# A 32-head attention layer and its feed-forward part on one core: output product from float16 pairs, first head by tiles, bounds' transfers on ScalarE's queue, new orders

## The chip, the core and the metric

The kernel runs on one core of a Trainium2 chip. A core has a matmul engine (TensorE, PE in the profile), a vector engine (VectorE, DVE), a scalar engine (ScalarE, ACT), a general engine (GpSimd, POOL) and a queue engine (SyncE, SP) that here issues nothing but transfers. Each engine works through its own instructions strictly in order, and they wait for one another by semaphores. The matmul engine reads its operands from the on-chip memory SBUF and writes to the accumulator memory PSUM, from which VectorE and ScalarE fetch the results. The metric is the device time of one execution in microseconds (us).

## The reference, cut to what matters

```python
x = hidden_states                       # (1, 1024, 512) float32
q  = layernorm(x) @ wq                  # 32 heads; 128 of each head's 192 columns are used
k, v = layernorm(x) @ wkv               # 32 heads of 128 each
probs = softmax(causal(q @ k.T * 192 ** -0.5))
x = x + (probs @ v for all heads, side by side) @ wo      # wo: (4096, 512)
h = relu(s0 * (layernorm(x) @ w0)) * 2  # w0, w1, w2: (512, 512) of +1 and -1
h = relu(s1 * (scaled(h) @ w1)) * 2
out = x + s2 * (scaled(h) @ w2)
```

## The kernel before

Tokens stand in 8 tiles of 128 (NT), and in 2 halves of 512 (NC). Every product is made from pairs: an operand is split into a high part (its float16 rounding) and a low part (the rest), and high by high, high by low and low by high are added up in PSUM. So a product of 128 contracted rows is 3 matmuls. Only the output product of attention (`project_out`, tiles `wos` and `attn`) and the feed-forward part use pairs of float32r values, which are four bytes wide.

The heads go in 16 groups of two (`GH`, `j` is the head in its group). Per head there are: seven products of the Strassen-Winograd scheme for q and k (`x1` to `x7`, 6 matmuls of 512 columns each), eight rows of scores (`s0` to `s7`, 128 to 1024 columns wide, 3 matmuls per 512 columns), four projections of values (`v`, 12 matmuls of 256 columns, eight a group since they serve both heads), two products of probabilities and values (`pv0`, `pv1`: 12 and 24 matmuls), and eight output tiles (`o0` to `o7`, 3 matmuls of 512 columns). In lots of 512 columns a group is 84 + 54 + 48 + 54 + 48 = 288.

Around them work: VectorE finds a score row's scaled minimum (`m`, line 968), takes the low part of the exponentials (`l`, line 975), gathers the products into q and k (`a`, line 907), takes the low part of values (`v`, line 952) and of attention (`pv`, line 958), adds the output to the residual (`o`, line 991), and works out a power of two by which the weights are scaled (`sc`, lines 930 to 941). ScalarE does exponentials (`e`, 706), high parts (`h` 714, `qk` 699, `v` 720, `pv` 728), the copy of the first product (`snap`, 655), sums of squares of the weights (`mx`, 688) and their scaling (`r`, 674). GpSimd splits the weights (`wqk`, `wv`, `wo`: lines 484, 487, 542, 545), forms the sums of weights of the scheme (`sum`, ten instructions), and the low parts of q and k (`qk`, 536). SyncE loads weights, transposes the probabilities by DMA (`t`, 460), and sends the sums of squares to DRAM and back, spread over the partitions (`put`, 405, `get`, 412).

What stands in which place on each engine is written out by hand as five tables of words (`TENSOR_ORDERS` and so on): `o7@-1` is output tile 7 of the head before the group's first, `x2@2` product 2 of the head two further on. The first string is the group that repeats, the second what stands ahead of group 0. Scores use two halves of one part of PSUM in turn (`psS`): row n waits for `l` of row n-2. All other products share four banks (`psC`), handed out by `BANKS` in the order of the products: a product waits in `bank_free` until whoever fetches the bank's last contents is done, with `a`, `snap`, `v`, `pv` or `o`.

## Time and profile before

| | us |
|---|---|
| median of 3 runs | 1137.72 |
| lowest, highest | 1137.38, 1139.09 |
| the profiled execution's own time | 1138.74 |
| its span in the trace | 1136.9 |
| PE busy in it | 1092.0 |
| DVE, ACT, POOL busy | 895.9, 678.0, 667.6 |

A matmul's duration in the trace includes the time until its result has drained, and the next one starts before it ends. So PE's pace is read from starts, not from durations, and its idle time is a little more than what the trace calls idle. Instructions of VectorE and ScalarE overlap a little too: a follower that waits for nothing starts about 0.08 to 0.10 us ahead of the end of the one before it.

### The profile page before, as it was taken

To read this page: it belongs to the slowest core of one execution; us is meant where nothing else is said; L and a number is where in the kernel's file an instruction comes from. 1 tells how busy PE (TensorE), PEld (TensorE's weight loads), DVE (VectorE), ACT (ScalarE), POOL (GpSimd) and SP (SyncE) were. 2 spreads that over 40 slices of the span, in tenths; PEclk is the share of its full clock that TensorE was granted. 3 is DMA by queue.
4 is the path that set the end of the run, shared out by engine and by line. 5 is a ranking of instruction groups with operands and counts; after the bars stand their busy time and mean duration, and the time that the engine had idled before them with its cause. 6 is when DMAs were issued, how large, how long until landed. Compare 5 with 4: busy or idle time off the path is not lost.

```text
span 1136.9 us, 18752 instructions
## 1 busy us (share of the span) xinstructions
PE 1092.0 (96%) x6223; PEld 655.2 (58%) x6223; DVE 895.9 (79%) x1797; ACT 678.0 (60%) x1334; POOL 667.6 (59%) x682
## 2 busy tenths in 40 slices
...
GB/s 157 88 99 84 119 108 128 100 116 94 96 112 109 121 114 114 82 117 109 91 121 114 124 82 119 112 76 121 117 130 89 117 107 81 118 93 115 92 1 75
DMA packets 367584, 118.25 MB, mean 104 GB/s; under 512 B 313088, under 2 KB 361344, under 8 KB 367488
## 3 DMA queue, kind: packets, MB, share of 16 engines
...
q8 instruction: 50, 0.82, 0.3%
q14 instruction: 46, 0.38, 0.2%
...
## 4 chain that ended last, share of the span: by engine, by line
PE 75%; DVE 12%; issue 6%; ACT 4%; POOL 3%; DMA 0%; SPq 0%; POOLq 0%; ACTq 0%; DVEq 0%
PE psC L1108 42%; PE psS L1108 16%; PE psC L1231 16%; DVE p L975 3%; DVE qk L907 2%; POOL wqk L487 2%; ACT raw L674 2%; POOL wqk L484 1%; DVE res L991 1%; DVE attn L958 1%; ACT attn L728 1%; DVE bound L930 1%; DVE psS L968 0%; DVE bound L936 0%; DVE bound L933 0%
## 5 line engine op out<-in xcount | busy, mean ns | idle before, releaser
L1108 PE MATMUL psC<-xb,wqk 128*128 128x512 f16 x1356 | 328.1, 381 | 12.5 <-POOL wqk L487 10.9
L706 ACT ACTIVATE psS<-psS,negmax 128x128 f32<-128x128 f32 (+7 forms) x256 | 182.8, 714 | 221.3 <-DVE negmax L968 220.4
L1108 PE MATMUL psC<-wos,attn 128*128 128x512 f32 x768 | 253.5, 441 | 13.5 <-DVE attn L958 10.1
L968 DVE CUSTOM_DVE_ANT_0 psS<-psS,mask,undo_qk 128x128 f32<-128x128 f32 (+7 forms) x256 | 208.4, 820 | 62.2 <-PE psS L1108 60.5
L975 DVE SCALAR_TENSOR_TENSOR p<-psS,p 128x128 f16<-128x128 f32 (+7 forms) x256 | 192.6, 752 | 60.2 <-ACT p L714 57.1
L1108 PE MATMUL psS<-qkT 128*128 128x512 f16 (+3 forms) x1152 | 230.0, 327 | 1.2 <-DVE p L975 0.7
L1108 PEld LDWEIGHTS psC<-xb,wqk 128*128 128x128 f16 x1356 | 124.5, 98 | 160.3 <-issue 36.3
L1231 PE MATMUL psC<-pT,v 128*128 128x512 f16 (+3 forms) x1152 | 197.8, 326 | 0.0
L991 DVE SCALAR_TENSOR_TENSOR res<-psC,rinv,res 128x512 f32<-128x512 f32 x256 | 190.1, 743 | 9.3 <-DVE rinv L982 8.1
L1108 PE MATMUL psC<-wvs,xb 128*128 128x256 f16 x1536 | 188.5, 273 | 0.4 <-POOL wvs L487 0.4
L484 POOL TENSOR_TENSOR wqk<-raw,one 128x512 f16<-128x512 f32 x122 | 115.9, 950 | 110.4 <-ACT raw L674 97.8
L714 ACT ACTIVATE p<-psS 128x128 f16<-128x128 f32 (+7 forms) x256 | 166.3, 649 | 17.9 <-DMA pT<-p 0.3
L1108 PEld LDWEIGHTS psC<-wos,attn 128*128 128x128 f32 x768 | 137.2, 190 | 63.4 <-issue 22.9
L536 POOL TENSOR_TENSOR qkT<-qk,qkT 128x512 f16<-128x512 f32 x120 | 137.1, 1158 | 59.6 <-ACT qkT L699 59.6
L1108 PEld LDWEIGHTS psC<-wvs,xb 128*128 128x128 f16 x1536 | 147.6, 98 | 35.8 <-issue 4.4
L1231 PEld LDWEIGHTS psC<-pT,v 128*128 128x128 f16 x1152 | 108.6, 98 | 91.5 <-DVE qk L907 4.1
L1108 PEld LDWEIGHTS psS<-qkT 128*128 128x128 f16 x1152 | 97.8, 98 | 102.9 <-issue 34.4
L487 POOL TENSOR_TENSOR wqk<-raw,wqk 128x512 f16<-128x512 f32 x124 | 129.1, 1041 | 15.8 <-ACT wqk L693 6.2
L484 POOL TENSOR_TENSOR wvs<-raw,one 128x512 f16<-128x512 f32 x45 | 46.8, 1040 | 119.3 <-ACT raw L674 82.3
L907 DVE SCALAR_TENSOR_TENSOR qk<-psC,qk 128x512 f32<-128x512 f32 x120 | 95.5, 816 | 10.0 <-PE psC L1108 8.4
L699 ACT ACTIVATE qkT<-qk 128x512 f16<-128x512 f32 x120 | 73.5, 625 | 38.2 <-DVE qk L907 38.2
L720 ACT ACTIVATE v<-psC 128x256 f16<-128x256 f32 x128 | 48.6, 381 | 62.0 <-PE psC L1108 62.0
...
## 6 DMA issues: line engine op xcount, KB each, us to landing
...
pT<-p SPq DMA_TRANSPOSE x256, 4.3
wrow<-wmax_rows SPq DMA_DIRECT2D x45, 64.0 KB, 4.7
...
```

The lines of the kernel that those rows point to most:

```text
L484: nc.gpsimd.tensor_tensor(hi, src, one[:, :].to_broadcast([P, src.shape[1]]), ALU.mult) \
L487: nc.gpsimd.tensor_tensor(lo, src, hi, ALU.subtract).then_inc(lo_sem, 1)
L536: nc.gpsimd.tensor_tensor(lo, qk32[:, AT[n], :], hi, ALU.subtract) \
L699: nc.scalar.activation(qkT[:, qk_slot(j, n), HI, :], qk32[:, AT[n], :], ACT.Copy) \
L706: nc.scalar.activation(row, row, ACT.Exp, bias=negmax[:, n:n + 1], scale=-1.0, accum_out=rowsum[:, j % 2, n:n + 1]) \
L714: nc.scalar.activation(parts_of(n)[:, :, HI, :], psS[:, n % 2, 0:(n + 1) * P].rearrange("p (k s) -> p k s", s=P), ACT.Copy, scale=UP).then ...
L907: nc.vector.scalar_tensor_tensor(to, product, OUT_DOWN, base32, ALU.mult, ALU.add).then_inc(gathered[n], 1)
L968: nc.vector.tensor_tensor_reduce(row, row, mask[:, S - width:S], undo_qk[:, j % 2:j % 2 + 1], 3e38, ALU.add, ALU.min, negmax[:, n:n + 1]). ...
L975: nc.vector.scalar_tensor_tensor(parts[:, :, LO, :], psS[:, n % 2, 0:(n + 1) * P].rearrange("p (k s) -> p k s", s=P), UP, parts[:, :, HI, ...
L991: nc.vector.scalar_tensor_tensor(res[:, t, :], psC[:, bank, :], rinv[:, t:t + 1], res[:, t, :], ALU.mult, ALU.add).then_inc(added, 1)
L1108: last = nc.tensor.matmul(out_ap, w, x, start=k == 0, stop=k == len(terms) - 1)
L1231: last = nc.tensor.matmul(o, a, b, start=(kt == 0 and k == 0), stop=(kt == count - 1 and k == 2))
```

## The change

- The output product reads float16 pairs. `wos` and `attn` are float16. The weights of the output are now scaled by a power of two as those of q, k and v are: their sum of squares (`mx2`), the bound (shared with that of the values, two columns at once) and the scaling (`r2`) come on top. ScalarE first copies a `pv` product to a float32 tile (`pv`, which frees the bank), then makes the high part from it (`ah`); the low part (`al`) goes from VectorE to GpSimd. The factor that undoes the scaling moves into the inverse of the row sums (one more small instruction per head on VectorE).
- `put` and `get` move from SyncE's queue to ScalarE's. Both output weights of a pair are loaded together.
- The first head's q and k are made tile by tile (128 columns) for four of the eight products, each as soon as its tile of x is there, and 34 matmuls whose results nobody reads are put ahead of the first transposes.
- All the orders are new, and so are the banks.

```diff
--- before.py
+++ after.py
...
 TENSOR_ORDERS = ("""
-    pv1@-1 s4@0 v0@0 s5@0 v1@0 x3@1 v2@0 s6@0 v3@0 x4@1 s7@0 x5@1 o4@-1 x6@1 o5@-1 x7@1 v4@0 o6@-1 x1@2 v5@0 s0@1
...
+    pv1@-1 x3@1 s4@0 x4@1 s5@0 x5@1 o4@-1 x6@1 s6@0 x7@1 s7@0 v0@0 o5@-1 v1@0 o6@-1 v2@0 s0@1 v3@0 x1@2 x2@2 o7@-1
+    pv0@0 s1@1 v4@0 s2@1 v5@0 s3@1 v6@0 o0@0 v7@0 s4@1 o1@0 s5@1 o2@0 pv1@0 o3@0 s6@1 x3@2 o4@0 s7@1 o5@0 o6@0 x4@2
...
-    m0@0 o0@-1 m1@0 l0@0 o1@-1 l1@0 a2@1 o2@-1 m2@0 m3@0 l2@0 l3@0 o3@-1 m4@0 m5@0 pv1@-1 l4@0 a3@1 v0@0 v1@0 v2@0
...
+    m5@0 l4@0 a5@1 o4@-1 l5@0 m6@0 a6@1 m7@0 a7@1 sc0@2 v0@0 l6@0 o5@-1 v1@0 v2@0 m0@1 o6@-1 rv0@0 v3@0 l7@0 m1@1
+    l0@1 a2@2 l1@1 m2@1 o7@-1 m3@1 v4@0 l2@1 v5@0 l3@1 v6@0 o0@0 o1@0 v7@0 m4@1 m5@1 l4@1 o2@0 l5@1 o3@0 m6@1 o4@0
...
+CHAINS = ("x", "ya", "yb", "y", "v", "pv", "o")
+
+TILED = {("ya", 0): 0, ("yb", 0): 1, ("ya", 4): 2, ("yb", 4): 3}
 NB = 4
 
-BANKS = "301230123012301201230120123012301230123012"
+WARM = (10, 24)
+
+BANKS = "230123012012301201230123012301230123012301"
...
-        attn = sb("attn", [P, 2, CH], F32R)
+        attn = sb("attn", [P, 2, CH], F16)
+        attn32 = sb("attn32", [P, 2, CH], F32)
...
-        wos = sb("wos", [P, 2, D], F32R)
+        wos = sb("wos", [P, 2, D], F16)
...
-        def load_out(q, h):
-            q.dma_start(raw[:, 4, :], wo_v[:, bass.ds(h, 1), :].rearrange("p a d -> p (a d)")) \
-                .then_inc(loaded["o"], 16)
+        def load_out(q, pair):
+            for k in range(GH):
+                q.dma_start(raw[:, 6 + k, :], wo_v[:, bass.ds(pair * GH + k, 1), :].rearrange("p a d -> p (a d)")) \
+                    .then_inc(loaded["o"], 16)
...
+            if n:
+                wait_pair(q, rows_max[1], g, 1, j, 1)
+                q.sem_inc(turn_go, 1)
+                wait_pair(q, rows_max[2], g, 1, j, 1)
+                q.dma_start(wpair_dram, wmax[:, 2:4]).then_inc(rows_out[1], 16)
+            else:
+                wait(q, rows_max[0], g, 1, j, 1)
+                q.dma_start(wmax_dram[j % 2:j % 2 + 1, :].rearrange("a p -> p a"), wmax[:, j % 2:j % 2 + 1])                     .then_inc(rows_out[0], 16)
...
+            if n:
+                wait_pair(q, rows_out[1], g, 16, j, 16)
+                q.dma_start(wrow_pair[:, :, :].rearrange("p r a -> p (r a)"),
+                            wpair_dram.rearrange("r a -> (r a)").partition_broadcast(P)).then_inc(rows_in[1], 16)
+            else:
+                wait(q, rows_out[0], g, 16, j, -16)
+                q.dma_start(wrow[:, j % 2, :], wmax_dram[j % 2, :].partition_broadcast(P)).then_inc(rows_in[0], 16)
...
-                wait(pool, loaded["o"], g, 16, j, 16)
+                wait_pair(pool, scaled[2], g, 1, j, 1)
                 wait(pool, done["o"], g, 8, j, 0)
-                nc.gpsimd.tensor_tensor(wos[:, HI, :], raw[:, 4, :], one[:, :].to_broadcast([P, D]), ALU.mult) \
-                    .then_inc(wo_hi, 1)
-                wait(pool, wo_hi, g, 1, j, 1)
-                nc.gpsimd.tensor_tensor(wos[:, LO, :], raw[:, 4, :], wos[:, HI, :].bitcast(F32), ALU.subtract) \
-                    .then_inc(wo_lo, 1)
+                split(raw[:, 6 + j % 2, :], wos[:, HI, :], wos[:, LO, :], wo_hi, wo_lo, lambda: wait(pool, wo_hi, g, 1, j, 1))
+
+            def attention_lo(g, j, c):
+                wait(pool, hi_done["pv"], g, 2, j, c + 1)
+                nc.gpsimd.tensor_tensor(attn[:, LO, :], attn32[:, c, :], attn[:, HI, :], ALU.subtract)                     .then_inc(lo_done["pv"], 1)
...
+                if n == 2 and isinstance(g, int) and g + j // GH == 0:
+                    act.wait_ge(bounded[2], 4)
+                    at, src = 3, raw[:, 6:8, :]
+                elif n:
                     wait_pair(act, bounded[1], g, 4, j, 4)
-                    at, src = 2, raw[:, 5:7, :]
+                    at, src = 1 + n, raw[:, 2 + 2 * n:4 + 2 * n, :]
                 else:
                     wait(act, bounded[0], g, 5, j, 4)
                     at, src = j % 2, raw[:, j % 2 * 2:j % 2 * 2 + 2, :]
                 src = src.rearrange("p a s -> p (a s)")
-                nc.scalar.activation(src, src, ACT.Copy, scale=bound[:, at, 3:4]).then_inc(scaled[n], 1)
...
-            def pv_hi(g, j, c, bank):
+            def keep_pv(g, j, c, bank):
                 wait(act, done["pv"], g, 2, j, c + 1)
+                wait(act, lo_done["pv"], g, 2, j, c - 1)
+                nc.scalar.activation(attn32[:, c, :], psC[:, bank, :], ACT.Copy, scale=PV_DOWN).then_inc(pv_kept, 1)
+
+            def attention_hi(g, j, c):
+                wait(act, pv_kept, g, 2, j, c + 1)
                 wait(act, done["o"], g, 8, j, 4 * c)
-                if j % GH == 0 and c == 0:
-                    wait_pair(act, undo_ready, g, 1, j, 1)
-                nc.scalar.activation(attn[:, HI, :], psC[:, bank, :], ACT.Copy, scale=undo_v[:, :]) \
+                nc.scalar.activation(attn[:, HI, :], attn32[:, c, :], ACT.Copy) \
                     .then_inc(hi_done["pv"], 1)
...
+                first = isinstance(g, int) and g + j // GH == 0
+                a, b = (j % 2, j % 2 + 1) if n == 0 else (n + 1, n + 2) if first else (2, 4)
+                done_n, per = bounded[n], 5 if n == 0 else 4
                 w = wait_pair if n else wait
-                total, root, inverse, scale = (bound[:, at, k:k + 1] for k in range(4))
-                if isinstance(g, int) and (GH * g + j <= 1 or n and g + j // GH == 0):
+                total, root, inverse, scale = (bound[:, k, a:b] for k in range(4))
+                if isinstance(g, int) and (n == 0 and GH * g + j <= 1 or n == 1 and first):
                     k = (0, 2)[GH * g + j] if n == 0 else 1
                     dve.wait_ge(spread_done, k + 1)
                     rows = psC[:, 3, k * P:(k + 1) * P]
                 else:
-                    w(dve, rows_in[n], g, 16, j, 0 if n else -16)
-                    rows = wrow[:, at, :]
+                    w(dve, rows_in[min(n, 1)], g, 16, j, 16 if n else -16)
+                    rows = wrow_pair[:, :, a - 2:b - 2].rearrange("p r a -> p a r") if n else wrow[:, a:b, :]
...
-                wait_pair(dve, lo_done["pv"], g, 2 * GH, j, 0)
-                nc.vector.tensor_scalar_mul(undo_v[:, :], bound[:, 2, 1:2], 2.0 ** (67 - W_UP) / UP).then_inc(undo_ready, 1)
+                if isinstance(g, int) and g + j // GH == 0:
+                    dve.wait_ge(bounded[2], 4)
+                wait(dve, rinv_done, g, 1, j, 0)
+                nc.vector.scalar_tensor_tensor(undo_o[:, :], bound[:, 1, 2:3], 2.0 ** (141 - 2 * W_UP), bound[:, 1, 3:4],
+                                               ALU.mult, ALU.mult).then_inc(undo_ready, 1)
...
-            def pv_lo(g, j, c, bank):
-                hi, lo = (attn[:, w, :] for w in (HI, LO))
-                wait(dve, hi_done["pv"], g, 2, j, c + 1)
-                nc.vector.scalar_tensor_tensor(lo, psC[:, bank, :], undo_v[:, :], hi.bitcast(F32), ALU.mult,
-                                               ALU.subtract).then_inc(lo_done["pv"], 1)
...
-                nc.vector.reciprocal(rinv[:, :], rowsum[:, j % 2, :]).then_inc(rinv_done, 1)
+                nc.vector.reciprocal(rowinv[:, :], rowsum[:, j % 2, :]).then_inc(inverse_done, 1)
+                wait(dve, inverse_done, g, 1, j, 1)
+                wait_pair(dve, undo_ready, g, 1, j, 1)
+                nc.vector.tensor_scalar_mul(rinv[:, :], rowinv[:, :], undo_o[:, :]).then_inc(rinv_done, 1)
...
-                    wait(pe, lo_done["pv"], g, 2, j, n + 1)
+                    wait(pe, pv_kept, g, 2, j, n + 1)
...
+            def plain_tile(step, t, bank):
+
+                n = TILED[step, t - t % 4]
+                c, a = n // 2 % 2, (A11, S2)[n % 2]
+                if t % 4 == 0:
+                    pe.wait_ge(plain_lo if n % 2 else first_lo, 1)
+                pe.wait_ge(xt_lo, t + 1)
+                terms = []
+                for d in range(DC):
+                    terms += halves(lambda w: wqk[:, w, a + d // 2, d % 2, :],
+                                    lambda w: xb[:, 2 * c + d // 2, w, d % 2, t % 4 * P:(t % 4 + 1) * P])
+                last = chain(psC[:, bank, t % 4 * P:(t % 4 + 1) * P], terms)
+                if t % 4 == 3:
+                    last.then_inc(plain_done, 1)
...
+            for t in range(WARM[0]):
+                nc.tensor.matmul(psT[:, t % 4, 0:P], ident[:, :], ident[:, :], start=True, stop=True)
             spread(0)
+            for t in range(WARM[1]):
+                nc.tensor.matmul(psT[:, t % 4, 0:P], ident[:, :], ident[:, :], start=True, stop=True)
             for t in range(4):
```

Three places of the order, in the group that repeats. First TensorE, from the second product of the head two further on (`x2@2`) to the following scores and values; `wqk` are weights of q and k, `wos` those of the output, `wvs` those of v, `psS` are scores, and what an instruction waits for stands in brackets. Before:

```order
L1108 MATMUL psC<-xb,wqk 128x512 [waits added]
L1108 MATMUL psC<-xb,wqk 128x512 x5
L1108 MATMUL psC<-wos,attn 128x512 [waits x1_kept]
L1108 MATMUL psC<-wos,attn 128x512 x2
L1108 MATMUL psS<-qkT 128x256 [waits p_lo]
L1108 MATMUL psS<-qkT 128x256 x2
L1231 MATMUL psC<-pT,v 128x512 [waits turned2,turned3,turned1,v_lo,turned0]
```

After, from the end of `pv0@0`:

```order
L1288 MATMUL psC<-pT,v 128x128 x3
L1149 MATMUL psS<-qkT 128x256 [waits p_lo]
L1149 MATMUL psS<-qkT 128x256 x2
L1149 MATMUL psC<-wvs,xb 128x256 [waits wv_lo,gathered2]
L1149 MATMUL psC<-wvs,xb 128x256 x11
L1149 MATMUL psS<-qkT 128x384 [waits p_lo]
L1149 MATMUL psS<-qkT 128x384 x2
L1149 MATMUL psC<-wvs,xb 128x256 [waits added]
L1149 MATMUL psC<-wvs,xb 128x256 x11
```

The scores `s1@1` now stand right ahead of `v4@0`, which waits for `gathered2` (the `a2@2` of VectorE), and `s2@1` right ahead of `v5@0`, which waits for `added` (the `o7@-1`).

VectorE at the same place: `psS,negmax` is `m`, `p` is `l`, `qk<-psC,x` is `a2`, `res` is `o`. Before:

```order
L968 ISA psS,negmax<-psS,mask,undo_qk 128x128 [waits s_done,bounded_qk]
L968 ISA negmax 128x1
L975 SCALAR_TENSOR_TENSOR p<-psS,p 128x128 [waits p_hi]
L907 SCALAR_TENSOR_TENSOR qk<-psC,x 128x512 [waits qk_lo0,x1_kept,x_done]
L968 ISA psS,negmax<-psS,mask,undo_qk 128x256 [waits s_done]
L968 ISA negmax 128x1
L991 SCALAR_TENSOR_TENSOR res<-psC,rinv,res 128x512 [waits added,o_done]
```

After:

```order
L1009 ISA psS,negmax<-psS,mask,undo_qk 128x256 [waits s_done]
L1009 ISA negmax 128x1
L1016 SCALAR_TENSOR_TENSOR p<-psS,p 128x128 [waits p_hi]
L949 SCALAR_TENSOR_TENSOR qk<-psC,x 128x512 [waits qk_lo0,x1_kept,x_done]
L1016 SCALAR_TENSOR_TENSOR p<-psS,p 128x2x128 [waits p_hi]
L1009 ISA psS,negmax<-psS,mask,undo_qk 128x384 [waits s_done]
L1009 ISA negmax 128x1
L1035 SCALAR_TENSOR_TENSOR res<-psC,rinv,res 128x512 [waits added,o_done]
```

`a2@2` stood ahead of `m1@1` and now stands behind it and behind `l0@1`; `o7@-1` stood behind `m1@1` and now stands behind `m2@1`.

GpSimd, from the split of an output weight to the sums; `attn` is the new `al`. Before:

```order
L542 TENSOR_TENSOR wos<-raw,one 128x512 [waits o_done,loaded_o]
L545 TENSOR_TENSOR wos<-raw,wos 128x512 [waits wo_hi]
L536 TENSOR_TENSOR qkT<-qk,qkT 128x512 [waits gathered7,qk_hi2]
L536 TENSOR_TENSOR qkT<-qk,qkT 128x512 [waits gathered6,qk_hi1]
L536 TENSOR_TENSOR qkT<-qk,qkT 128x512 [waits gathered5,qk_hi3]
L515 TENSOR_TENSOR raw<-raw 128x256 [waits first_lo]
```

After:

```order
L515 TENSOR_TENSOR wos<-raw,one 128x512 [waits o_done,scaled_o]
L518 TENSOR_TENSOR wos<-raw,wos 128x512 [waits wo_hi]
L515 TENSOR_TENSOR wqk<-raw,one 128x512 [waits x_done,scaled_qk]
L518 TENSOR_TENSOR wqk<-raw,wqk 128x512 [waits first_hi]
L577 TENSOR_TENSOR attn<-attn 128x512 [waits pv_hi]
L567 TENSOR_TENSOR qkT<-qk,qkT 128x512 [waits gathered5,qk_hi3]
L567 TENSOR_TENSOR qkT<-qk,qkT 128x512 [waits gathered7,qk_hi2]
L546 TENSOR_TENSOR raw<-raw 128x256 [waits first_lo]
```

Between an output weight's split and the low part of attention there is now the split of the next head's first weights, and both qkT steps and the sums follow on that.

## Rows read from the trace of the kernel before

**Rows 1.** Windows, one group: us; busy (instructions) by engine; clock, DMA share, GB/s

```profile
454.19:519.84 65.65, 64.41 (x372) 37.95 (x373) 52.48 (x106) 39.66 (x80) 42.68 (x44) 1.00 0.56 108
```

**Rows 2.** Waits of PE, whole span: us in total, times, longest us

```profile
PE psC L1108 <- POOL wqk L487: 10.9, 15, 1.3
PE psC L1108 <- DVE attn L958: 10.1, 18, 2.3
```

**Rows 3.** Timeline of PE: start us, us, line, count of one kind

```profile
544.01 1.47 PE L1108 MATMUL psC<-xb,wqk 128*128 128x512 f16 x6
...
546.01 2.76 PE L1108 MATMUL psC<-xb,wqk 128*128 128x512 f16 x12
```

**Rows 4.** Timeline of PE, DVE, ACT, POOL in turn, 511.6 to 520 us

```profile
511.67 1.46 PE L1108 MATMUL psC<-xb,wqk 128*128 128x512 f16 x6
...
519.84 0.38 PE L1108 MATMUL psC<-xb,wqk 128*128 128x512 f16 x1 [0.69 <-POOL wqk L487]
...
511.88 1.29 DVE L968 CUSTOM_DVE_ANT_0 psS<-psS,mask,undo_qk 128x1024 f32<-128x1024 f32 x1 [0.27 <-PE psS L1108]
...
515.31 0.28 DVE L930 TENSOR_REDUCE bound<-wrow 128x1 f32<-128x128 f32 x1
...
516.13 0.74 DVE L991 SCALAR_TENSOR_TENSOR res<-psC,rinv,res 128x512 f32<-128x512 f32 x1
...
516.19 1.15 ACT L674 ACTIVATE raw<-raw,bound 128x1024 f32<-128x1024 f32 x1 [0.68 <-DVE bound L938]
...
517.41 1.04 POOL L484 TENSOR_TENSOR wqk<-raw,one 128x512 f16<-128x512 f32 x1 [5.74 <-ACT raw L674]
518.53 1.17 POOL L487 TENSOR_TENSOR wqk<-raw,wqk 128x512 f16<-128x512 f32 x1
```

**Rows 5.** Groups by form, DVE: busy us, mean ns of one

```profile
L991 DVE SCALAR_TENSOR_TENSOR res<-psC,rinv,res 128x512 f32<-128x512 f32 x256 | 190.1, 743 | 9.3 <-DVE rinv L982 8.1 <-PE psC L1108 0.6
L952 DVE SCALAR_TENSOR_TENSOR v<-psC,v 128x256 f16<-128x256 f32 x128 | 52.1, 417 | 36.4 <-ACT v L720 36.4
L907 DVE SCALAR_TENSOR_TENSOR qk<-psC,x 128x512 f32<-128x512 f32 x60 | 41.0, 684 | 2.8 <-PE psC L1108 2.8
L975 DVE SCALAR_TENSOR_TENSOR p<-psS,p 128x896 f16<-128x896 f32 x32 | 34.5, 1078 | 0.4 <-ACT p L714 0.4
L968 DVE CUSTOM_DVE_ANT_0 psS<-psS,mask,undo_qk 128x384 f32<-128x384 f32 x32 | 19.7, 617 | 0.0
L941 DVE SCALAR_TENSOR_TENSOR undo_qk<-bound 128x1 f32<-128x1 f32 x32 | 19.0, 595 | 0.0
L968 DVE CUSTOM_DVE_ANT_0 psS<-psS,mask,undo_qk 128x256 f32<-128x256 f32 x32 | 15.4, 481 | 0.0
L975 DVE SCALAR_TENSOR_TENSOR p<-psS,p 128x128 f16<-128x128 f32 x32 | 9.2, 288 | 15.6 <-ACT p L714 15.6
```

**Rows 6.** Groups by form, ACT and POOL

```profile
L655 ACT ACTIVATE x<-psC 128x512 f32<-128x512 f32 x30 | 17.9, 595 | 1.6 <-PE psC L1108 0.3
...
L536 POOL TENSOR_TENSOR qkT<-qk,qkT 128x512 f16<-128x512 f32 x120 | 137.1, 1158 | 59.6 <-ACT qkT L699 59.6
```

**Rows 7.** Timeline of POOL, first and last of the ten instructions of sums

```profile
461.61 0.72 POOL L515 TENSOR_TENSOR raw<-raw 128x256 f32<-128x256 f32 x1
...
469.38 1.16 POOL L487 TENSOR_TENSOR wqk<-raw,wqk 128x512 f16<-128x512 f32 x1
```

**Rows 8.** Timeline of SP's queue, a put and its get, 30 to 70 us

```profile
32.61 0.34 SPq L405 DMA_DIRECT2D wmax_rows<-wmax  x1
...
39.78 0.34 SPq L412 DMA_DIRECT2D wrow<-wmax_rows  x1
```

**Rows 9.** The page's DMA issues: count, KB each, median us to landing

```profile
wrow<-wmax_rows SPq DMA_DIRECT2D x45, 64.0 KB, 4.7
```

**Rows 10.** Timeline of the start: first chains of q and of v

```profile
17.98 4.38 PE L1108 MATMUL psC<-xb,wqk 128*128 128x512 f16 x12 [1.63 <-DVE xb L867]
...
28.11 4.10 PE L1108 MATMUL psC<-wvs,xb 128*128 128x256 f16 x36 [0.36 <-POOL wvs L487]
```

More of the change, by code:

```diff
@@ L100, in exists @@
         return False
-    if h == 0 and (step[0] in ("mx", "sc", "r", "put", "get", "lqk", "lv") or step[0] == "wv" and step[2] == 2):
+    if h == 0 and (step[0] in ("lqk", "lv") or step[0] in ("mx", "sc", "r", "put", "get") and step[2] == 0 or step[0] == "wv" and step[2] == 2):
         return False
@@ L123, in group_steps @@
             return [x for x in every if x not in gone]
-        return [x for x in steady if exists(g, x)]
+        late = [("pv", -1, 1), ("ah", -1, 1)] + [("o", -1, t) for t in range(4, 8)]
+        return [x for x in steady if exists(g, x) and x not in late] + [x for x in late if x in steady]
     return [x for x in steady if exists(g, x) and x not in done]
@@ L141, in plan_banks @@
             if step not in CHAINS:
+                continue
+            if step in ("ya", "yb") and n % 4:
+                plan[g, step, j, n] = (plan[g, step, j, n - n % 4][0], None)
                 continue
@@ L181, in bank_at, with plain_step @@
     raise AssertionError((step, j, n))
+def plain_step(j, n):
+    return (("ya", "yb")[n % 2], j, n // 2 * 4) if n < 4 else ("y", j, n)
 def rows_of(i):
@@ L213, in build @@
     UP = 2.0 ** 15
+    PV_DOWN = 2.0 ** -25
     INH = -4.0
@@ L258, in build @@
         scl2 = sb("scl2", [P, 3], F32)
-        wmax = sb("wmax", [P, 3], F32)
-        squares = sb("squares", [P, 3, 2 * 512], F16)
-        wrow = sb("wrow", [P, 3, P], F32)
-        bound = sb("bound", [P, 3, 4], F32)
+        wmax = sb("wmax", [P, 4], F32)
+        squares = sb("squares", [P, 4, 2 * 512], F16)
+        wrow = sb("wrow", [P, 2, P], F32)
+        wrow_pair = sb("wrow_pair", [P, P, 2], F32)
+        bound = sb("bound", [P, 4, 4], F32)
         undo_qk = sb("undo_qk", [P, 2], F32)
-        undo_v = sb("undo_v", [P, 1], F32)
-        wmax_dram = nc.dram_tensor("wmax_rows", (3, P), F32).ap()
+        undo_o = sb("undo_o", [P, 1], F32)
+        wmax_dram = nc.dram_tensor("wmax_rows", (2, P), F32).ap()
+        wpair_dram = nc.dram_tensor("wmax_pair", (P, 2), F32).ap()
         w_all = sb("w_all", [P, 3, DC, D], F32R)
@@ L598, in pool_steps @@
                         split_out(g, j)
+                    elif step == "al":
+                        attention_lo(g, j, n)
                     elif step == "qk":
@@ L788, in _ @@
             ends = group_steps(SCALAR_ORDERS, NG)
-            assert ends[-1] == ("pv", -1, 1)
-            for step in ends[:-1]:
+            assert ends[-2:] == [("pv", -1, 1), ("ah", -1, 1)]
+            for step in ends[:-2]:
                 scalar_step(NG, *step)
             norm_root(2)
+            scalar_step(NG, *ends[-2])
             scalar_step(NG, *ends[-1])
@@ L1056, in _ @@
             outs = [x for x in ends if x[0] == "o"]
-            late = ends[ends.index(("pv", -1, 1)):]
-            early = [x for x in ends if x not in late]
-            assert [x[2] for x in late[1:]] == [4, 5, 6, 7]
+            late = ends[-4:]
+            early = ends[:-4]
+            assert late == [("o", -1, t) for t in range(4, NT)]
             for t in range(4):
```

111 lines of the change are left out of this document (54 added, 57 removed).

## Prediction

> **What bounds the kernel now.** I read the table of busy shares first (PE 1092.0 of 1136.9 us), then the windows of one group, then PE's waits, then timelines of single stretches. A group takes 65.65 us, the same step starting at 454.19 and at 519.84, and PE is busy for 64.41 of it [rows 1]. So PE bounds the kernel, and the rest is short waits. A group has 288 lots of 512 columns. The pace of float16 is read from starts: in a chain of 12 that lasts 2.76 us, with 0.38 for the last, the starts are (2.76 - 0.38) / 11 = 0.216 us apart [rows 3]. That makes 62.2 us. Six float16 matmuls and three of the output product take 546.01 - 544.01 = 2.00 us [rows 3], while nine at 0.216 take 1.944, so a chain of the output costs 0.056 more than in float16, and 16 of them 0.9. Left are 65.65 - 62.2 - 0.9 = 2.5 us a group, some 2.3 of waits and 0.2 of small things. The list of waits names only half of that (15 times GpSimd's `wqk`, 18 times VectorE's `attn`) [rows 2], since a matmul's duration covers the first 0.16 us.
>
> One of these waits shows how all are to be computed. From the end of `s7@0` at 511.67 to the start of `x1@2` at 519.84 are 8.17 us, and PE's own work there is 7.3 (four steps of 1.30, three of 0.65, 3 x 0.056) [rows 4]. The other way from the same end: VectorE starts `m7` 0.21 later, works on to the bound, begun at 515.31, ScalarE scales from 516.19, GpSimd splits from 517.41 in two steps 1.12 apart, done at 519.70, and PE starts 0.14 later [rows 4]. The difference, 0.87 us, is the wait. It follows from the order of two engines and from durations, and comes back in each group. So for the new order I look for steps of PE that wait for something which its own engine does only behind a thing that needs PE's step just before.
>
> **What float16 saves.** 0.9 us a group, about 14 us in all if nothing else takes its place.
>
> **What the new order waits for.** A follower on VectorE starts 0.08 us ahead of the other's end; its first start is 0.21 behind PE's end, and PE starts 0.06 behind a result. Each of these chains starts at an end on PE, and I take off what PE does meanwhile.
>
> A, `v4@0` behind `s1@1`. Its bank is freed by `a2@2`, which stands behind `m1@1` and `l0@1`, and `m1@1` needs the scores PE has just made. 0.21 + 0.40 (`m1`, 0.481 less 0.08) + 0.21 (`l0`, 0.288 less 0.08) + 0.68 (`a2`) + 0.06 = 1.56 us [rows 5], in which PE has nothing to do. `l0` also needs `h0@1`, which ScalarE now does behind the copy of `pv0@0` (0.60, as the nearest copy from PSUM to float32 [rows 6]): that makes 1.63.
>
> B, `v5@0` behind `s2@1`. Its bank is freed by `o7@-1`, behind `m2@1`: 0.21 + 0.53 + 0.74 + 0.06 = 1.55 us [rows 5].
>
> C, `v2@0`, `v1@0`. After `s7@0` VectorE does `m7` 1.21, `a7` 0.60, the bound (516.13 - 515.31 = 0.82), `v0` 0.34, `l6` 1.00, `o5` 0.74: with 0.21 and 0.06 that is 4.98 us, and 5.25 since `v0` first needs ScalarE's high part behind `qk2@1` [rows 4, 5]. PE has `v0 o5 v1 o6`, 3.90. So 1.1 to 1.35; I take 1.3. One step in it, line 941, takes 0.595 on average [rows 5], though all five of the bound took 0.82 at 515.31: about every second one is held up by roughly 0.9, and this one falls at the moment at which GpSimd starts `qk2@1`. I add 0.3 for that, with 0 and 0.95 as bounds.
>
> D, `o0@1`. From the end of `o7@0` GpSimd splits the output weight and the next first weight (four steps of 1.12 [rows 4]) and makes the low part of attention (1.16, as the same form for qkT [rows 6]): with starts and ends 5.9 us. PE has `x5 pv0 x6 x7`, 5.5. Wait 0.4.
>
> E, `x3@1`. From there GpSimd does two qkT steps (2.24) and the sums, 469.38 + 1.16 - 461.61 = 8.93 us [rows 7], 11.2 in all; PE has 11.0, and by way of `a7` the chain is 0.15 longer. Wait 0.3, bounds 0 and 0.5.
>
> None of these can cover another, because each begins at an end on PE that lies behind the last wait. Sum 1.63 + 1.55 + 1.6 + 0.4 + 0.3 = 5.5 us a group against 2.3 now. The new group is 62.2 + 0.2 + 5.5 = 67.9 us, 2.25 more than 65.65. All of it comes in 14 groups and part of it in the first and last; times 14.5 that is 32.6 us. The lower bound of the waits is 1.56 + 1.5 + 1.1 + 0.3 + 0 = 4.45, a period of 66.85, and 17 us in all.
>
> Cost nothing: ScalarE's added copies (4 of 0.6 us a group), scaling and squares, since it is busy 39.66 of 65.65 us [rows 1] and only A and C hang on its place; `al` apart from D, since its slack elsewhere on GpSimd is above a microsecond; the doubled bound on VectorE, behind which `m5` stands, and `s6@0` keeps some 0.7 us; SyncE, which loses put and get, since PE's list has no wait for a transpose [rows 2]. If these margins go, PE waits for the difference.
>
> On line 941 the Trainium skill has a rule, in "SBUF — State Buffer", section "SBUF: two separate sides": VectorE with two SBUF inputs and GpSimd share a pair of ports that the first to start holds for its whole instruction. The trace agrees with it (0.595 on average for a 0.15 us step). By it C would be 1.3 or 2.3, nothing between.
>
> **Start and end.** The first chain of q starts at 17.98 and takes 4.38 us for 12 matmuls, against 2.76 at the usual pace [rows 3, 10]; with PE kept running this 1.6 should go, unless the matmuls ahead last beyond the first transposes. By tiles, q can start up to 2 us earlier. Scaling the value weights earlier brings the first `v` from 28.11 [rows 10] to about 24, but then VectorE's sums of x bound the first 60 us, and they remain. Between -8 (all of it kept) and -1 I take -4, nearest to what the 1.6 and the 2 add up to. The end: float16 saves some 1.5 us, two copies and GpSimd's step ahead of the last output tiles cost as much; 0, bounds -1.5 and 1.5.
>
> Sum on the profiled execution: 1138.7 + 32.6 - 4 = 1167.3; the median of the runs lies 1.0 below it, so 1166.
>
> **Rivals.** First, slower still, by ScalarE's own queue. A put was issued at 32.61 and its get could not start before 39.78, though little else was moving [rows 8]: 7.1 us. `get1@0` now comes some 5.6 us behind `put1@0` (an estimate from the durations of `e0` to `e3` and PE's steps between), so ScalarE stands for 1.5 us or more with exponentials behind it. Those have slack; the landing 4.7 us later [rows 9] does not, since `sc1@0` on VectorE then comes up to 1.4 us late, and `s6@0` and `v0@0` with it. That adds up to 20 us: about 1183, chance 0.15. The Trainium skill ("DMA: Bandwidth & Descriptors", section "Anatomy of one DMA") gives one transfer, from another queue than this, a fixed cost of about 2 us; by that the get would not wait at all. The row says 7.1, and it decides.
>
> Second, faster. The waits of the new order are no longer than those of the old (2.3), because VectorE, relieved of four low parts of attention, gets ahead and the chains A and B are hidden somewhere I don't see. Then a group is 64.7 us, 0.95 less, times 15.5 is 15, and 5 at the start: 1118. For it speaks the relief, against it that A and B have nothing in them which an idle VectorE could do earlier. Chance 0.12.
>
> Third, about the same: waits at their lower bound (+17), and start and end at theirs (-9.5), 1145, and a little less again if C's bank is free sooner. Inside 0.2% (2.3 us, about what a measurement of this kernel tells from no change) is little: 0.03.
>
> Fourth, float16 doesn't quicken the chains: 0.9 us a group dearer, 1179, chance 0.05. It speaks for it only that both forms have 512 columns.
>
> My forecast has 0.65. Range: 1145 is the low bound as above; 1190 holds the first rival and C held up each time (1166 + 0.65 x 14.5 = 1175) together in part. Left out are the faster case and the tails. Faster 0.12, same 0.03, slower 0.85.
>
> **What the new profile would show.** PE's idle list headed by `psC` waiting for `qk L949` (A) and `res L1035` (B), each some 1.4 us as listed, 14 or 15 times; for `res L1035` again at `v2@0`; a short one for `attn L577`. The period from one `x1@2` to the next 67 to 69 us. Output matmuls 0.216 apart. PE's first chain of q at full pace. I am wrong if A or B is missing, if the period is under 65.65, or if ScalarE shows waits of microseconds for `wmax_pair`.

## The result and the profile after

The changed kernel takes 1248.35 us (median of 4 runs, 1246.25 to 1260.88) against 1138.4 for the kernel before on the same chip: ratio 1.0988, 95% interval 1.096 to 1.1016. It is slower, as forecast, but by 110 us and not by 28; 1166 was predicted, and 1248 lies far outside 1145 to 1190.

The page of the profiled run (1249.42 us) shows more busy time of TensorE than before (1092.0) though float16 was to save some, and a granted clock that is no longer full everywhere:

```profile
span 1247.6 us, 19455 instructions
...
PE 1112.9 (89%) x6435; PEld 622.9 (50%) x6435; DVE 877.0 (70%) x1769; ACT 738.3 (59%) x1446; POOL 734.8 (59%) x746
...
PEclk9999999989999998999999998999989999999999
```

The row that answers to [rows 1], one group from one `v4@0` to the next (the same columns): 73.77 us, about 1 us more than the mean, and the granted clock 0.95:

```profile
437.35:511.12 73.77, 66.30 (x372) 35.46 (x373) 51.19 (x103) 43.52 (x87) 47.04 (x48) 0.95 0.61 97
```

From `v4@0` of the second group to that of the fifteenth, 13 groups, are 946.7 us, 72.8 a group (before: 853.4 us, 65.65 a group). 67.9 was predicted.

TensorE's waits, answering to [rows 2] (us in total, times, longest):

```profile
PE psC L1288 <- DMA pT<-p: 48.2, 16, 4.2
PE psC L1149 <- DVE res L1035: 31.0, 28, 1.4
PE psC L1149 <- DVE qk L949: 20.3, 14, 1.5
PE psC L1149 <- POOL attn L577: 11.3, 19, 2.7
```

Rows two to four are the chains B and C, A, and D of the prediction. The first row is new: `pv1@-1` waits for transposed probabilities. In the timeline, A and B stand as they were worked out. TensorE, around `s1@1 v4@0 s2@1 v5@0`:

```profile
435.41 0.49 PE L1149 MATMUL psS<-qkT 128*128 128x256 f16 x3
437.35 1.48 PE L1149 MATMUL psC<-wvs,xb 128*128 128x256 f16 x12 [1.45 <-DVE qk L949]
438.68 0.65 PE L1149 MATMUL psS<-qkT 128*128 128x384 f16 x3
440.71 1.49 PE L1149 MATMUL psC<-wvs,xb 128*128 128x256 f16 x12 [1.38 <-DVE res L1035]
```

Read from start to start, with the columns at 0.216 us per 512 taken off, the waits are 1.62 us (A, predicted 1.63) and 1.55 (B, predicted 1.55), in every group. C is 1.00 (predicted 1.3 and 0.3 for the port), D 0.57 (predicted 0.4), E is not there (predicted 0.3).

The new wait, one of fifteen, TensorE from the last scores to `pv1@-1` (first from a timeline up to 406 us, then the whole product):

```profile
402.11 0.81 PE L1149 MATMUL psS<-qkT 128*128 128x512 f16 x3
405.46 1.01 PE L1288 MATMUL psC<-pT,v 128*128 128x512 f16 x2 [2.54 <-DMA pT<-p]
```

```profile
405.46 5.91 PE L1288 MATMUL psC<-pT,v 128*128 128x512 f16 x24 [2.54 <-DMA pT<-p]
```

Read from starts it is 2.70 us. What was it waiting for? VectorE finished the low part of the head's last row (1024 wide, the second line here) at 397.40:

```profile
393.16 1.08 DVE L1016 SCALAR_TENSOR_TENSOR p<-psS,p 128x896 f16<-128x896 f32 x1
...
396.18 1.22 DVE L1016 SCALAR_TENSOR_TENSOR p<-psS,p 128x1024 f16<-128x1024 f32 x1
```

SyncE issued the transpose `t7@-1` at 397.49, at once, and `t6@-1` at 394.33, at once behind the row above it. A usual transpose has landed 3.8 us later (median of the page). ScalarE's queue had `put0@2` at 393.62 and `put1@0` at 398.52:

```profile
393.62 0.33 ACTq L434 DMA_DIRECT2D wmax_rows<-wmax  x1
...
398.52 0.33 ACTq L431 DMA_DIRECT2D wmax_pair<-wmax  x1
```

The view of one line in a window shows when each of the four landed. In order of issue, `put0@2`, `t6@-1`, `t7@-1`, `put1@0`:

```profile
L434 ACTq DMA_DIRECT2D wmax_rows<-wmax x1: 327/327/327, 393.6 to 393.6; - x1
...
DMA to landing us min/median/max: 7.9/7.9/7.9
```

```profile
L491 SPq DMA_TRANSPOSE pT<-p x1: 1537/1537/1537, 394.3 to 394.3; - x1
...
DMA to landing us min/median/max: 7.4/7.4/7.4
```

```profile
L491 SPq DMA_TRANSPOSE pT<-p x1: 2886/2886/2886, 397.5 to 397.5; - x1
...
DMA to landing us min/median/max: 7.8/7.8/7.8
```

```profile
L431 ACTq DMA_DIRECT2D wmax_pair<-wmax x1: 326/326/326, 398.5 to 398.5; - x1
...
DMA to landing us min/median/max: 6.6/6.6/6.6
```

So `put0@2` lands at 401.51 and `t6@-1` at 401.70; `put1@0` lands at 405.15, `t7@-1` at 405.32, and TensorE starts at 405.46. `t7@-1` lands 0.16 to 0.21 us behind `put1@0` in each of the 15 groups, though the put is on another queue and is issued 1.0 to 1.5 us later. Over the run, the 63 transposes that had a put still under way 3.5 us after their issue have a median of 7.7 us, the other 193 one of 3.6. Not all of the 63 are that close behind a put: 22 landed within 0.25 us of it, the others up to 2.9 us later.

The Trainium skill states a rule that fits ("DMA: Bandwidth & Descriptors", section "Queues, rings and completion order"): a transfer's semaphore is a strongly ordered write, which lands only after every earlier write of that DMA engine, of its other queues too. The trace agrees for `t7@-1`, 0.2 us behind the put. But the rule speaks of when the semaphore is told, and the trace shows that the data come late as well. While `put0@2` is under way the DMA engines are busier and move less than a third: a DMA share of 1.39 and 56 GB/s (the last two columns of the first row), against 0.95 and 180 at the same place in the run in which the puts are cut to one row (the second row, from the first experiment below). In 14 groups the same 3 us have 19 to 77 GB/s against 175 to 180.

```profile
398.50:401.50 3.00, 3.00 (x20) 1.59 (x19) 2.34 (x7) 1.94 (x7) 2.76 (x5) 1.00 1.39 56
```

```profile
381.50:384.50 3.00, 3.00 (x20) 1.63 (x19) 2.33 (x7) 1.96 (x7) 2.77 (x5) 1.00 0.95 180
```

Why so few bytes of a put slow the packets of the transposes, no run here shows.

And TensorE pays twice. Three windows of it, the wait, what follows, and a little later (the clock stands ahead of the last two columns):

```profile
402.70:405.40 2.70, 0.22 (x2) 0.00 (x0) 2.40 (x6) 1.45 (x4) 2.62 (x3) 0.96 1.04 106
405.40:407.00 1.60, 1.54 (x4) 0.58 (x5) 0.56 (x1) 0.49 (x1) 1.52 (x2) 0.50 0.11 4
409.00:411.00 2.00, 2.00 (x13) 1.08 (x12) 0.00 (x0) 0.00 (x0) 0.00 (x0) 1.00 0.94 224
```

Behind the wait the granted clock is 0.50, which is 1.2 GHz of 2.4, and 7 to 14 matmuls run at 0.43 us per 512 columns. That happened behind all 14 waits of 2.17 us and more, and not behind the one of 0.87 us; it adds up to some 27 us. The waits themselves are 50 us from start to start.

### The profile page after: what moved, and what is told of

Same layout as the page of the kernel before. It is cut to its first block, busy times and chain, and to the rows that moved or that the text cites. A ratio compares the mean times of both kernels' runs of the same rounds, so it can differ in the third digit from the quotient of the medians.

```text
span 1247.6 us, 19455 instructions
## 1 busy us (share of the span) xinstructions
PE 1112.9 (89%) x6435; PEld 622.9 (50%) x6435; DVE 877.0 (70%) x1769; ACT 738.3 (59%) x1446; POOL 734.8 (59%) x746
## 4 chain that ended last, share of the span: by engine, by line
PE 71%; DVE 12%; DMA 7%; issue 4%; ACT 3%; SPq 2%; POOL 0%; DVEq 0%; POOLq 0%; ACTq 0%
PE psC L1149 41%; PE psC L1288 17%; PE psS L1149 13%; DMA pT<-p 7%; DVE p L1016 3%; SPq L491 2%; DVE psS L1009 2%; DVE res L1035 2%; DVE qk L949 1%; ACT qkT L735 1%; ACT v L756 0%; DVE rinv L1026 0%; ACT psS L742 0%; DVE negmax L1009 0%; PE psS L1330 0%
## 5 line engine op out<-in xcount | busy, mean ns | idle before, releaser
L1149 PE MATMUL psC<-xb,wqk 128*128 128x512 f16 (+1 forms) x1500 | 325.9, 359 | 1.4 <-DVE xb L909 1.3
L1288 PE MATMUL psC<-pT,v 128*128 128x512 f16 (+3 forms) x1152 | 224.3, 353 | 50.0 <-DMA pT<-p 48.2
L1149 PE MATMUL psC<-wos,attn 128*128 128x512 f16 x768 | 205.7, 382 | 11.3 <-POOL attn L577 11.3
L1149 PEld LDWEIGHTS psC<-xb,wqk 128*128 128x128 f16 x1500 | 137.7, 98 | 133.8 <-issue 2.4
L577 POOL TENSOR_TENSOR attn<-attn 128x512 f16<-128x512 f32 x64 | 74.0, 1157 | 219.2 <-ACT attn L767 219.2
L1288 PEld LDWEIGHTS psC<-pT,v 128*128 128x128 f16 x1152 | 115.1, 103 | 172.9 <-issue 77.3
L750 ACT ACTIVATE p<-psS 128x128 f16<-128x128 f32 (+7 forms) x256 | 165.8, 648 | 32.5 <-DMA wmax_pair<-wmax 15.3
L1149 PEld LDWEIGHTS psS<-qkT 128*128 128x128 f16 x1152 | 107.6, 98 | 111.9 <-DVE p L1016 17.3
L1149 PEld LDWEIGHTS psC<-wos,attn 128*128 128x128 f16 x768 | 71.0, 98 | 82.9 <-issue 20.8
L762 ACT ACTIVATE attn<-psC 128x512 f32<-128x512 f32 x64 | 38.2, 598 | 121.1 <-PE psC L1288 121.1
L949 DVE SCALAR_TENSOR_TENSOR qk<-psC,x 128x512 f32<-128x512 f32 x60 | 41.1, 685 | 92.6 <-PE psC L1149 92.6
```

Source lines behind the costliest of these rows:

```text
L577: nc.gpsimd.tensor_tensor(attn[:, LO, :], attn32[:, c, :], attn[:, HI, :], ALU.subtract) .then_inc(lo_done["pv"], 1)
L750: nc.scalar.activation(parts_of(n)[:, :, HI, :], psS[:, n % 2, 0:(n + 1) * P].rearrange("p (k s) -> p k s", s=P), ACT.Copy, scale=UP).then ...
L949: nc.vector.scalar_tensor_tensor(to, product, OUT_DOWN, base32, ALU.mult, ALU.add).then_inc(gathered[n], 1)
L1149: last = nc.tensor.matmul(out_ap, w, x, start=k == 0, stop=k == len(terms) - 1)
L1288: last = nc.tensor.matmul(o, a, b, start=(kt == 0 and k == 0), stop=(kt == count - 1 and k == 2))
```

## The experiments

Theory 1: the puts, where they now stand, hold the transposes `t6@-1` and `t7@-1`, and `pv1@-1` waits for them, then runs at half clock because TensorE stood still. Theory 2: it is SyncE's own queue, where `lo0@0` waits up to 9.4 us for the splits of the output weights with `t6@-1` behind it. Each experiment starts from the changed kernel except where it says otherwise.

**Puts of one row.**

```diff
+                r = P if g + j // GH < 2 else 1
-                q.dma_start(wpair_dram, wmax[:, 2:4]).then_inc(rows_out[1], 16)
+                q.dma_start(wpair_dram[0:r, :], wmax[0:r, 2:4]).then_inc(rows_out[1], 16)
```

and the same for `wmax_rows` from the fifth head on.

> From the third pair of heads on, a put sends 4 or 8 bytes of one partition in place of all 128; the other sums in DRAM stay those of an earlier head. Nothing else changes. Theory 1 (in the changed kernel the puts, issued at 393.6 and 398.5 us and landed 7.9 and 6.6 us later, hold the transposes t6 and t7 that are under way, which land within 0.2 us behind them, and pv1@-1 on TensorE waits for these): the 48 us of waits for pT go to under 8, the 27 us of half pace behind them go too, so 1248 - 50 - 27 = 1171 us, between 1160 and 1185. Theory 2 (SyncE's own queue: the load lo0@0 waits up to 9.4 us for the splits of the output weights, and t6 and t7 stand behind it): no change, 1245 to 1251.

Measured: 1178.66 us (ratio 1.0354, 1.0335 to 1.0374). The waits for transposes are down to two; the other chains are what they were:

```profile
PE psC L1151 <- DVE res L1037: 31.0, 28, 1.4
PE psC L1151 <- DVE qk L951: 20.3, 14, 1.5
PE psC L1151 <- POOL attn L579: 10.9, 19, 2.7
PE psS L1151 <- DVE p L1018: 7.5, 5, 4.0
PE psC L1290 <- DMA pT<-p: 3.2, 2, 2.6
```

Theory 1 holds, and theory 2 falls: SyncE's order was not changed, and its wait for the splits of the output weights stayed as long as it was (after, then this run), while TensorE's wait went.

```profile
SPq L416 <- POOL wos L518: 127.8, 15, 9.4
```

```profile
SPq L416 <- POOL wos L520: 127.0, 15, 9.3
```

`t7@-1`, which landed 8.7 us after its issue (median of the groups), now lands after 4.2, though the put still comes 1.0 us behind it. The 13 groups now take 879.5 us, 67.65 each, where the prediction, which knew nothing of the hold, had 67.9.

**The loads of output weights later.** In `SYNC_ORDERS`:

```diff
-t5@-1 lo0@0 t6@-1 t7@-1 t0@0
+t5@-1 t6@-1 t7@-1 lo0@0 t0@0
```

> In SyncE's order the loads of the output weights (lo0@0) stand behind t7@-1 instead of ahead of t6@-1. Theory 2 (SyncE's queue): t6 and t7 are issued several us earlier, the waits of pv1@-1 for pT and the half pace behind them go, about 1171 us. Theory 1 (puts): no gain, since t6 was issued only when its low part l6 was done, 1.0 us behind the loads; 1240 to 1260, a little slower where the sums of squares of the output weights (mx2) and put1 come later.

Measured: 1336.37 us (1.175, 1.1712 to 1.1788), far slower than either theory had it. ScalarE's queue shows why, and TensorE's waits what followed:

```profile
ACT squares L724 <- DMA raw<-in_L_attn_wo: 138.0, 15, 10.8
```

```profile
PE psS L1149 <- DVE p L1016: 133.3, 19, 10.2
```

`mx2@0` stands in the middle of ScalarE's order and waits for the loads, with the exponentials of the next head behind it. I had written "a little slower"; it was 9 us a group. The loads had no room to move, and the place of a load is a place on ScalarE too. Since the put behind `mx2@0` moved with the loads, this run decides nothing between the theories.

**The puts later, nothing left out.** In `SCALAR_ORDERS` and `VECTOR_ORDERS`:

```diff
-ah0@-1 put0@2 qk3@0 qk2@0 qk1@0 mx2@0 put1@0 e0@0 snap0@1 h0@0 e1@0 h1@0 e2@0 e3@0 get1@0 h2@0 pv1@-1 h3@0 get0@2 ah1@-1 e4@0 h4@0 r1@0 e5@0
+ah0@-1 qk3@0 qk2@0 qk1@0 mx2@0 e0@0 snap0@1 h0@0 e1@0 h1@0 put1@0 put0@2 e2@0 e3@0 h2@0 pv1@-1 h3@0 ah1@-1 get1@0 get0@2 e4@0 h4@0 e5@0 r1@0
-a4@1 sc1@0 m5@0 l4@0 a5@1
+a4@1 m5@0 l4@0 sc1@0 a5@1
```

> Nothing is left out. In ScalarE's order put0@2 and put1@0 move behind h1@0, some 3 us behind the issue of t7@-1, their gets behind ah1@-1, r1@0 behind e5@0, and on VectorE sc1@0 moves behind l4@0. Theory 1: the waits for pT and the half pace go (-77 us). Put1 then lands at about 11 us behind s3@0's start instead of where get1 stood, the value weights are split about 0.6 us late (0 to 3 us) for v0@0, 9 us in all (0 to 45): 1180 us, 1165 to 1215. Theory 2: 1248 or more.

Measured: 1200.84 us (1.055, 1.0534 to 1.0565). No wait for a transpose is left in TensorE's list. What took its place, ScalarE, then TensorE:

```profile
ACT psS L742 <- DMA wmax_rows<-wmax: 41.9, 13, 3.7
...
PE psC L1149 <- POOL wvs L518: 14.9, 15, 1.0
```

ScalarE now stands 3.2 us at `get0@2`, for `put0@2`, with its exponentials behind it. That is the mechanism of the prediction's first rival, brought about by this edit and at the other pair of put and get; in the changed kernel itself the wait is for `put1@0`, 15.3 us in 12 times, and costs TensorE nothing that its list shows. How long a put takes is not fixed either: here `put1@0`, of 128 pieces, lands after 3.9 us in the median (3.4 to 5.7), and `put0@2`, issued 0.4 us behind it, after some 10.

**VectorE's order alone.**

```diff
-l7@0 m1@1 l0@1 a2@2 l1@1 m2@1 o7@-1 m3@1
+l7@0 a2@2 m1@1 l0@1 o7@-1 l1@1 m2@1 m3@1
```

> VectorE's order alone: a2@2 stands ahead of m1@1 and o7@-1 ahead of l1@1 and m2@1, as it could be in the idle 2.1 us that VectorE shows there. The prediction's chains A and B: the excess of 1.62 us ahead of v4@0 and of 1.55 ahead of v5@0 goes in each group, 3.17 x 15 = 47 us, 1201 us (1195 to 1210), the waits for pT remaining as they are. Rival (what is won there is given back at pv1@-1, since t6 and t7 land at a time that TensorE's pace does not set): 1225 to 1245.

Measured: 1218.23 us (1.0705, 1.0663 to 1.0746), between the two. A and B are gone from the list, so they were what the prediction said. But of 47 us only 30 are kept:

```profile
PE psC L1288 <- DMA pT<-p: 55.4, 16, 6.1
...
PE psC L1288 <- DVE v L999: 8.5, 9, 1.7
```

The waits for transposes grew from 48.2 to 55.4 us: a transfer that lands at a time of its own takes back what is won ahead of it. The second line, in which `pv1` waits for VectorE's low part of the values, was 1.0 us and takes back another 7.5.

**The later puts, VectorE's order, and `l6@0` behind `o5@-1` (chain C), together.**

> The later puts, the new VectorE order of the last two runs together, and l6@0 behind o5@-1 (chain C, 1.0 us a group). Nothing is left out. If what each took away adds up: 1201 - 47 - 2 = 1152 us (chain C is down to 0.15 us in the run with later puts). If ScalarE's wait for put1 (3.2 us each) now comes nearer to the end of TensorE's slack, less is kept: up to 1180. Range 1145 to 1180.

Measured: 1161.44 us (1.0203, 1.0173 to 1.0234), inside the range and 9 above the sum. What remains is ScalarE's wait at the get, which is for `put0@2` and not, as I had written ahead of the run, for `put1@0`, and `wvs` (14.9 us). I take TensorE's 26.9 us of waits for VectorE's low parts to be what the get's wait costs; that link was not followed in the timeline.

**TensorE kept at work in the wait.** In `values`, ahead of the waits for transposes:

```diff
+                if c == 1 and j % 2 == 1 and g < NG:
+                    for k in range(16):
+                        nc.tensor.matmul(psC[:, bank, :], v[:, HI, 0, 0:P], xb[:, 0, HI, 0, :], start=True, stop=True)
```

> The changed kernel with 16 more matmuls of 512 columns (3.45 us at 0.2156 us each) ahead of pv1@-1 in each group, into its bank, whose result is overwritten. Nothing is left out. TensorE then works where it stood waiting for pT. If the half pace of the 7 to 14 matmuls behind that wait (27 us in all; granted clock 0.50 in the stretch 405.4 to 407.0) comes from its having stood still, it goes: 1248 - 27 + 6 (where the wait was under 3.45 us) = 1227 us, 1218 to 1236. If it comes from what the matmuls read or from the transfers under way, it stays: 1250 to 1258.

Measured: 1236.3 us (1.0846, 1.0814 to 1.0879), 0.3 above the range. The profiled execution is the fastest of the four, 1229.4 us. Its granted clock is 0.999 over the whole of it (0.993 to 0.996 in the other three, where some of the loss may be left), and at the same place (406 to 408 us, `pv1@-1` at work):

```profile
406.00:408.00 2.00, 2.00 (x12) 0.97 (x11) 2.00 (x3) 0.40 (x1) 1.92 (x3) 1.00 0.86 164
```

Inside the `pv` products 0.3 us of excess is left between 250 and 1100 us where it was some 23. The `pv` products read the same operands and the same transfers go on, so the half pace came from TensorE's having stood still. 240 matmuls more made the kernel 12 us faster.

**The sums as rows, nothing left out.** VectorE turns the column of 128 sums into four rows of 32, and the put sends four pieces of 128 bytes:

```diff
+                    nc.vector.transpose(wmaxT[:, j % 2, :], wmax[:, j % 2, :]).then_inc(rows_turned[0], 1)
...
-                q.dma_start(wmax_dram[j % 2:j % 2 + 1, :].rearrange("a p -> p a"), wmax[:, j % 2:j % 2 + 1])
+                q.dma_start(wmax_dram[j % 2, :].rearrange("(b i) -> b i", i=32), wmaxT[0:P:32, j % 2, :])
```

> The changed kernel, nothing left out, with another way for the same sums: VectorE turns the column of 128 sums into 4 rows of 32 (32 by 32 blocks, one instruction a put), and a put sends 4 pieces of 128 bytes (8 for a pair) in place of 128 of 4 or 8 bytes. Theory 1 (a put holds the transposes for as long as its many small pieces take): as with one row, and the hold at 68 to 80 us in the first group goes as well (about 4 us): 1175 us, 1162 to 1185. Rival (a put holds them whatever its size, as each transfer to DRAM between transposes would): 1240 to 1255.

Measured: 1176.66 us (1.0334, 1.0317 to 1.0352). No transpose is held any longer, by the time to landing of all 256 (kernel before: 2.8/4.3/10.1; changed kernel: 2.3/3.8/11.8), and the turning costs 0.2 us each:

```profile
DMA to landing us min/median/max: 2.3/3.6/6.5
```

```profile
L1051 DVE STREAM_TRANSPOSE wmaxT<-wmax 128x32 f32<-128x32 f32 x30 | 6.0, 201 | 0.0
```

So it is the many small pieces of a put, and not a put as such. The puts also come 0.6 us later against `t7@-1` here, since they wait for VectorE's turn; the run with one row, which kept their place, rules that out as the cause. Whether it is the number of the pieces, their 4 or 8 bytes, or the number of DMA engines that share them, the two runs don't tell apart.

**The rows, VectorE's order and chain C together.**

> The sums by rows as in the last one, the VectorE order with a2@2 and o7@-1 earlier, and l6@0 behind o5@-1. Nothing left out. If chains A, B and C (1.62, 1.55 and 1.0 us a group) go and nothing takes their place: 1175 - 4.17 x 15 = 1112 us, faster than the kernel before (1138.5). If GpSimd's chains D and E, which the prediction put at 0.4 and 0.3 with little slack, take up part of it: up to 1140. Range 1105 to 1140.

Measured: 1116.41 us (0.9802, 0.9783 to 0.982), faster than both kernels, than the one before by 2.0%. A group takes 63.55 us, of which TensorE is busy 62.99 (before 65.65 and 64.41 [rows 1]):

```profile
389.40:452.95 63.55, 62.99 (x375) 34.97 (x373) 50.53 (x106) 43.16 (x87) 46.97 (x49) 1.00 0.60 113
```

**The kernel before with puts of one row.**

> The kernel before, with its puts cut to one partition from the third pair of heads on (the other sums stay those of an earlier head). If it is the place of the puts among the transposes that costs, and not puts as such, nothing is to be had here: its list of TensorE's waits names no transpose, so 1138.5 us, 1134 to 1141. Rival (the puts cost the kernel before too, by their hold on the transposes or by the gets behind them on SyncE): 1100 to 1130.

Measured: 1138.76 us (0.9997, 0.9988 to 1.0006). There the puts seem to hold transposes as well (one issued at 495.08, right behind a put, took 7.0 us; with one row the median of all fell from 4.3 to 3.6 us), but none that TensorE is about to need.

**GpSimd's low part of attention first**, from the fastest kernel:

```diff
-qk0@0 wo0@-1 wqk0@1 al0@-1
+qk0@0 wo0@-1 al0@-1 wqk0@1
```

> The fastest so far (sums by rows, a2@2 and o7@-1 earlier, l6@0 behind o5@-1; 1116.4 us), and on GpSimd al0@-1 ahead of wqk0@1 (chain D, excess 0.57 us ahead of o0@1 in each group). x1@3 stands 0.65 us behind o0@1 and needs wqk, whose two steps now end the chain: 0.57 - 0.65 is below nothing, so the whole 0.57 x 15 = 8.5 us goes: 1108 us, 1105 to 1113. Rival (x1@3 waits for wqk instead): 1116.

Measured: 1143.2 us (1.0043, 1.003 to 1.0055), 27 slower instead of 8 faster. I had overlooked what `al0@-1` itself waits for: `pv0@1`, which stands only three steps ahead of `o0@1` on TensorE. ScalarE fetches that product (the first two lines; `pv` is L1305), GpSimd stands until its high part is there, and `wqk` comes late. The name in GpSimd's own bracket is that of another product, long done:

```profile
423.36 0.60 ACT L767 ACTIVATE attn<-psC 128x512 f32<-128x512 f32 x1 [0.58 <-PE psC L1305]
423.99 0.63 ACT L772 ACTIVATE attn<-attn 128x512 f16<-128x512 f32 x1
```

```profile
424.69 1.16 POOL L579 TENSOR_TENSOR attn<-attn 128x512 f16<-128x512 f32 x1 [1.87 <-PE psC L1166]
```

```profile
PE psC L1166 <- POOL wqk L520: 26.3, 30, 1.4
```

**Without the 34 early matmuls**, from the fastest kernel (`WARM = (0, 0)`):

> The fastest so far without the 34 matmuls ahead of the first transposes. They end before the operands of the first transposes are there (1.28 us of idle behind them), so they delay nothing. Without them the 16 transposes and the first chains should run at half pace as in the kernel before (3.68 us for 16 in place of 2.02): later by 1 to 2 us: 1118 us, 1115 to 1121. Rival: the start is set by VectorE and ScalarE, which then hide it all: 1116.

Measured: 1126.17 us (0.9892, 0.9878 to 0.9905), 10 slower, which neither side had. The second group's `v4@0` stands only 0.5 us later (135.6 against 135.1). The rest came in the groups: `pv1@-1` waits for transposes again, 0.2 to 0.9 us in each of 11 groups (the twelfth wait, 2.1 us at the end, is in the fastest kernel too):

```profile
PE psC L1305 <- DMA pT<-p: 7.5, 12, 2.1
```

So this doesn't price the early matmuls. `t7@-1` lands 6.0 us after its issue in place of 4.3 (medians), and the fastest kernel had only 0.9 to 1.5 us to spare there. The trace has something at that place that the fastest kernel has not: in all 15 groups one packet of the queue that the page calls `q8 instruction`, 0.9 us long, starts 2.5 to 3.0 us behind the issue of `t7@-1`; in the fastest kernel none of the 15 groups has one there. For 1.5 us behind it the data nearly stop (40 GB/s, clock, share and GB/s being the last three columns):

```profile
362.00:363.50 1.50, 1.37 (x8) 0.51 (x6) 1.03 (x3) 1.27 (x5) 1.34 (x3) 1.00 1.25 40
```

That leaving out 34 matmuls moves these packets to another place is my reading of it; no run moved them alone.

## Why the prediction was wrong

**What held.** The direction; that TensorE's own work and its waits bound the kernel; chains A and B to 0.02 us; the float16 pace (output matmuls start 0.2155 us apart). With the hold taken out, the period is 67.65 (one row) and 67.75 (rows) against 67.9. That it came so near is luck in part: C was 0.3 to 0.6 too long and E 0.3, D 0.2 too short, so that the chains are 4.7 us together where 5.5 stood, and 0.5 us of gaps of 0.2 us and less, for which the sum has no term, made up for it. The allowance for GpSimd's port in C was not needed.

**The step that failed** is in "Cost nothing": "SyncE, which loses put and get, since PE's list has no wait for a transpose [rows 2]". The list of the kernel before can't tell this. It says that no transpose was late where the transposes and puts stood then. The change moves `pv1@-1` to the head of the group with `t7@-1` issued only 5 us ahead, and puts `put0@2` and `put1@0` right around it. What the prediction put at nothing measured 67.2 us: in the 13 middle groups the changed kernel is 93.3 us longer than the one before, of which 67.2 are the hold and the half clock behind it (946.7 less 879.5) and 26.1 the waits that were predicted at 29.3.

**The row was there.** The put's 7.1 us [rows 8] was used for the first rival, for what the get behind it costs ScalarE. What else is under way in those 7 us was not asked, although transposes stand between that kernel's puts and gets, and the longest took 10.1 us to land. The first rival was the right transfer with the wrong victim. Its own sign did come, ScalarE's waits for `wmax_pair` (15.3 us in 12 times, the longest 2.0), but it was hidden: the run with one row has none of these waits, and TensorE waits for `p` 7.5 us in 5 times in both. Not tried is the new order with `put` and `get` back on SyncE's queue, so what the move to ScalarE's queue did by itself is not known.

**Two more, smaller.** A wait of microseconds was priced at its length; behind one of 2.2 us or more came half a clock, 1.9 us each on average. And the start: it and the end together are 17.4 us longer than before (8.7 in the kernel with rows), where -4 and one and a half groups of waits gave about -1. About 9 of that is the hold in the first two groups, where a transpose issued at 68.11 landed at 79.94 behind a put of 9.7 us. The other 9 are at the start. Counted in lots of 512 columns (the 34 early matmuls left out), TensorE of the changed kernel has done 100 lots after 46.0 us (before: 46.2) and 200 after 75.7 (before: 71.2): 4.5 us lost, where 4 were to be won and the bounds were 8 and 1. Between the two it waits 2.35 us for VectorE's low part, and the granted clock is 0.72 from 56 to 62 us:

```profile
56.18 1.97 PE L1149 MATMUL psS<-qkT 128*128 128x512 f16 x6 [2.35 <-DVE p L1016]
```

The kernel with rows has the same wait there (2.34 us) and is 4.9 us behind after 200 lots. The prediction had seen that VectorE bounds the first 60 us, and still gave the start 4 us.
